# Taking the last layer of one half and the first layer of the next in turn, in a four-layer graph network on one core

## The reference, cut to what matters

```python
h = maximum(layernorm(x), 0); x = x + L0(h, adj)   # attention: e = leaky(s1_i + s2_j), masked softmax, times h W
h = maximum(layernorm(x), 0); x = x + L1(h, adj)   # attention on edge scores (h*a) h^T, softmax, times h
h = maximum(layernorm(x), 0); x = x + L2(h, adj)   # sum over relations of (mask_r h) W_r, plus bias
h = maximum(layernorm(x), 0); x = x + L3(h, adj)   # as L0, then elu
```

## Time and profile before

| | us |
|---|---|
| median of 3 runs | 293.67 |
| lowest and highest | 293.42, 294.1 |
| the profiled execution | 293.83 |
| its span, first to last instruction | 292.0 |
| PE busy in it | 276.5 |
| ACT busy | 257.4 |
| DVE busy | 251.2 |
| POOL busy | 237.4 |

### The profile page before, as it was taken

One profiled execution on the slowest core, in us unless ns is written; L12 is line 12 of the kernel. 1 busy time (PEld: TensorE's weight loads), 2 busy tenths in 40 slices (PEclk: granted clock), 3 DMA queues, 4 the chain that ended last, 5 costly groups with the idle time before them and its releaser, 6 DMA issues.

```text
span 292.0 us, 8093 instructions
## 1 busy us (share of the span) xinstructions
PE 276.5 (95%) x2250; PEld 257.6 (88%) x2250; DVE 251.2 (86%) x1211; ACT 257.4 (88%) x850; POOL 237.4 (81%) x382
## 2 busy tenths in 40 slices
PE   1899999999999999999899999999999999999991
PEld 1799998899889999999878999989888999999991
DVE  2689998998988767999998799999898886799995
ACT  3799998899998887897999889799999988789993
POOL 6999875777657999999999887768765699999932
PEclk9999999999999999999999999999999999999998
DMA  7935554500000000012121470000000000001123
GB/s 198 324 80 185 179 169 142 137 28 1 2 0 3 0 2 3 2 36 75 36 75 37 125 276 2 3 0 2 1 2 1 3 0 0 2 4 37 56 90 113
DMA packets 15950, 17.79 MB, mean 61 GB/s; under 512 B 2720, under 2 KB 11808, under 8 KB 15904
## 3 DMA queue, kind: packets, MB, share of 16 engines
q1 hardware_dynamic: 15488, 17.18, 18.5%
q10 hardware_dynamic: 416, 0.07, 0.1%
HBM read 13.05 MB, written 4.19 MB: 59 GB/s over the span
## 4 chain that ended last, share of the span: by engine, by line
PE 77%; DVE 10%; ACT 7%; issue 2%; DMA 2%; POOL 1%; SPq 0%; ACTq 0%; DVEq 0%; POOLq 0%
PE bank L972 23%; PE bank L914 9%; PE bank L919 9%; PE bank L890 7%; PE bank L848 6%; PE bank L957 5%; PE bank L939 5%; PE bank L927 4%; PE bank L969 3%; DVE pT L675 3%; PE bank L921 2%; DVE expy L709 2%; PE bank L874 2%; DVE result L718 2%; DMA edges<-in_adj 2%
## 5 line engine op out<-in xcount | busy, mean ns | idle before, releaser
L354 POOL TENSOR_TENSOR rs<-mv,minus_half 128x2 f32<-128x2 f32 x128 | 92.5, 723 | 41.4 <-DVE mv L619 41.2
L972 PE MATMUL bank<-val,pT 128*128 128x129 f32 x512 | 74.6, 275 | 0.0
L972 PEld LDWEIGHTS bank<-val,pT 128*128 128x128 f32 x512 | 67.8, 193 | 0.0
L368 POOL TENSOR_TENSOR h<-h,rs 128x256 f32<-128x256 f32 x96 | 59.7, 621 | 0.2
L675 DVE SCALAR_TENSOR_TENSOR pT<-bank,val,edgesT 128x256 f32<-128x256 f32 x128 | 55.0, 470 | 1.9 <-issue 1.0
L608 DVE BATCH_NORM_STATS2 st<-x 128x6 f32<-128x128 f32 x192 | 43.5, 267 | 0.0
L511 ACT ACTIVATE val<-bank,val 128x128 f32<-128x128 f32 x128 | 42.4, 406 | 0.1
L890 PE MATMUL bank<-w_gat,hT 128*128 128x131 f32 x256 | 41.0, 284 | 0.6 <-ACT hT L479 0.6
L848 PE MATMUL bank<-ident,h 128*128 128x128 f32 x192 | 38.2, 281 | 1.9 <-POOL h L368 1.5
L362 POOL TENSOR_TENSOR h<-x,mv 128x256 f32<-128x256 f32 x64 | 39.7, 621 | 0.0
L969 PE MATMUL bank<-ident,vsum 128*128 128x128 f32 x128 | 35.5, 277 | 1.4 <-DVE x L701 0.8
(11 more groups left out here) (84 smaller groups left out, 661.5 us busy)
## 6 DMA issues: line engine op xcount, KB each, us to landing
edges<-in_adj SPq DMA_DIRECT2D x32, 256.0 KB, 3.7
xin<-in_x SPq DMA_DIRECT2D x32, 128.0 KB, 2.7
out_x<-result SPq DMA_DIRECT2D x32, 128.0 KB, 1.7
w_rel<-in_L_gnn_weight SPq DMA_DIRECT2D x1, 256.0 KB, 2.9
w_gat<-in_L_gnn_W ACTq DMA_DIRECT2D x1, 64.0 KB, 2.6
w_gat<-in_L_gnn_W SPq DMA_DIRECT2D x1, 64.0 KB, 3.4
a_rel<-in_L_gnn_a SPq DMA_DIRECT2D x4, 0.5 KB, 3.4
bias<-in_L_gnn_bias SPq DMA_DIRECT2D x1, 64.0 KB, 3.1
```

The costliest lines, as they stand in the source:

```text
L354: pool.tensor_tensor(rs[:, g % WIDE], mv[:, g % WIDE, :, 1], minus_half[:, :], ALU.pow).then_inc(rs_ready, 1)
L368: pool.tensor_tensor(h[:, n % HS, :, 0:D], h[:, n % HS, :, 0:D], rs[:, g % WIDE, :].rearrange("p (t o) -> p t o", o=1).to_broadcast([P, T, ...
L972: last = pe.matmul(bank_o(n)[:, t], pT[:, n % 4, u, t * P:(t + 1) * P], values[:, u], start=(u == 0 and layer == 1), stop=(u == T - 1), sk ...
```

## The change

`ORDER` is new in its middle. Layers 0 to 2 of graphs 0 to 15 stand as before, and layers 1 to 3 of graphs 16 to 31. Between them came 16 units of layer 3 and then 16 of layer 0; now come (3,0), (3,1), and then in turn two units of layer 3 and two of layer 0, (3,2) (3,3) (0,16) (0,17) (3,4) (3,5) (0,18) (0,19) and so on, with (0,30) (0,31) last. `BEHIND` = 2 says how far layer 3 leads.

Since units of two halves are now mixed, slots that went by graph go by unit: st, mv, rs, nb, rinv, sums by n % WIDE, val by n % SLOTS, expy and relu_y by the count of layer 3 units, hsum and vsum by `gat_slot(n)`. The third bank of O is given only where seven units of layer 3 stand in a row, thus in the last stage alone. `residual` of layer 0 in graphs 16 to 31 gets a wait for the result of the graph whose x1 it overwrites. The lists of stages of PE, ACT, DVE and POOL have new lags and a new order; SP's lags grow from 10 to 12.

```diff
+BEHIND = 2
-ORDER = [(layer, first + k) for first in range(0, B, WIDE) for layer in range(4) for k in range(WIDE)]
+ORDER = [(layer, k) for layer in range(3) for k in range(WIDE)] + [(3, k) for k in range(BEHIND)]
+for k in range(0, WIDE, 2):
+    if k + BEHIND < WIDE:
+        ORDER += [(3, k + BEHIND), (3, k + BEHIND + 1)]
+    ORDER += [(0, WIDE + k), (0, WIDE + k + 1)]
+ORDER += [(layer, WIDE + k) for layer in range(1, 4) for k in range(WIDE)]
-LAG_MAX = 13
-SP_LAG = 10
+LAG_MAX = 15
+SP_LAG = 12
-        third = layer == 3 and (n + 6 >= len(ORDER) or ORDER[n + 6][0] == 3)
+        third = all(later == 3 for later, _ in ORDER[n:n + 7])
+def gat_slot(n):
+
+    return (nth(GATS, n) - 1) % SLOTS
...
-                pool.tensor_tensor(rs[:, g % WIDE], mv[:, g % WIDE, :, 1], minus_half[:, :], ALU.pow).then_inc(rs_ready, 1)
+                pool.tensor_tensor(rs[:, n % WIDE], mv[:, n % WIDE, :, 1], minus_half[:, :], ALU.pow).then_inc(rs_ready, 1)
...
                 src = xin[:, g % XS] if layer == 0 else x1[:, g % WIDE]
-                for t in range(T):
-                    last = dve.scalar_tensor_tensor(x1[:, g % WIDE, t], bank_o(n)[:, t, 0:D], rinv[:, g % WIDE, t:t + 1],
+                if layer == 0 and g >= WIDE:
+                    dve.wait_ge(result_ready[g % 2], (g - WIDE) // 2 + 1)
+                for t in range(T):
+                    last = dve.scalar_tensor_tensor(x1[:, g % WIDE, t], bank_o(n)[:, t, 0:D], rinv[:, n % WIDE, t:t + 1],
                                                     src[:, t], ALU.mult, ALU.add)
...
-            pipeline([(put_o, 8, LAST), (put_o, 8, FIRST), (put_z, 6, RGCN_REL), (put_z, 5, MULTI_REL),
+            pipeline([(put_v, 5, LAST), (put_v, 5, FIRST), (put_z, 6, FIRST), (put_z, 6, RGCN_REL),
```

More of the change, by code:

```diff
@@ L457, in normalize @@
                 for t in range(T):
-                    last = act.activation(h[:, n % HS, t, 0:D], x1[:, g % WIDE, t], ACT.Relu, bias=nb[:, g % WIDE, t:t + 1],
-                                          scale=rs[:, g % WIDE, t:t + 1])
+                    last = act.activation(h[:, n % HS, t, 0:D], x1[:, g % WIDE, t], ACT.Relu, bias=nb[:, n % WIDE, t:t + 1],
+                                          scale=rs[:, n % WIDE, t:t + 1])
                 last.then_inc(h_ready, 1)
@@ L510, in scale_v @@
                 for t in range(T):
-                    last = act.activation(val[:, k, t, 0:D], bank_v(n)[:, t, 0:D], ACT.Copy, scale=val[:, k, t, D:D + 1])
+                    last = act.activation(val[:, n % SLOTS, t, 0:D], bank_v(n)[:, t, 0:D], ACT.Copy, scale=val[:, n % SLOTS, t, D:D + 1])
                 last.then_inc(v_ready, 1)
@@ L549, in elu_parts @@
                 for t in range(T):
-                    act.activation(expy[:, n % 4, t], bank_o(n)[:, t, 0:D], ACT.Exp, scale=rinv[:, g % WIDE, t:t + 1])
-                    last = act.activation(relu_y[:, n % 4, t], bank_o(n)[:, t, 0:D], ACT.Relu, scale=rinv[:, g % WIDE, t:t + 1])
+                    act.activation(expy[:, (nth(LAST, n) - 1) % 4, t], bank_o(n)[:, t, 0:D], ACT.Exp, scale=rinv[:, n % WIDE, t:t + 1])
+                    last = act.activation(relu_y[:, (nth(LAST, n) - 1) % 4, t], bank_o(n)[:, t, 0:D], ACT.Relu, scale=rinv[:, n % WIDE, t:t + 1])
                 last.then_inc(y_ready, 1)
[L554 to L557, removed]
-                      (elu_parts, 9, LAST), (mask_edges, 4, FIRST), (scale_hT, 4, MULTI_REL),
-                      (exponentials, 6, MULTI_REL)])
+            pipeline([(take_edgesT, 5, FIRST), (scale_v, 6, LAST), (take_hT, 4, FIRST),
+                      (scale_v, 6, FIRST), (take_hT, 4, MULTI_REL), (take_hT, 4, LAST),
+                      (take_pT, 8, MULTI_REL), (mask_edges, 3, FIRST), (exponentials_of_s, 5, FIRST),
+                      (scale_hT, 4, MULTI_REL), (exponentials_of_s, 5, LAST), (take_mh, 6, RGCN_REL),
+                      (elu_parts, 9, LAST), (normalize, 4, RGCN_REL), (exponentials, 6, MULTI_REL),
+                      (upper_part, 5, MULTI_REL)])
             act.wait_ge(flag_ready, 1)
@@ L607, in statistics @@
                 for t in range(T):
-                    last = dve.bn_stats(st[:, g % WIDE, t, 0:6], src[:, t])
+                    last = dve.bn_stats(st[:, n % WIDE, t, 0:6], src[:, t])
                 last.then_inc(stats_ready, 1)
@@ L867, in put_edgesT @@
                 before = [m for m in THIRD if m < n]
-                if before and g % WIDE == 0:
+                if before and g % WIDE == 0 and before[0] < n:
                     pe.wait_ge(y_ready, nth(LAST, before[-1]))
@@ L892, in put_v @@
                 if k % VB == VB - 1:
-                    last = pe.matmul(bank_vsum(n), w_gat[layer // 3][:, 0:D], hsum[:, k - VB + 1:k + 1], start=True, stop=True)
+                    last = pe.matmul(bank_vsum(n), w_gat[layer // 3][:, 0:D], hsum[:, gat_slot(n) - VB + 1:gat_slot(n) + 1], start=True, stop=True)
                 last.then_inc(v_put, 1)
@@ L974, in put_o @@
                 last.then_inc(o_put, 1)
-            pipeline([(put_o, 8, LAST), (put_o, 8, FIRST), (put_z, 6, RGCN_REL), (put_z, 5, MULTI_REL),
-                      (put_o, 8, RGCN_REL), (put_edgesT, 5, FIRST), (put_hT, 3, MULTI_REL),
-                      (put_z, 5, FIRST), (put_pT, 7, MULTI_REL), (put_v, 4, FIRST), (put_o, 8, MULTI_REL),
-                      (put_hT, 3, FIRST), (put_hT, 3, LAST), (put_v, 4, LAST), (put_z, 5, LAST)])
+            pipeline([(put_v, 5, LAST), (put_v, 5, FIRST), (put_z, 6, FIRST), (put_z, 6, RGCN_REL),
+                      (put_z, 6, LAST), (put_z, 5, MULTI_REL), (put_o, 8, RGCN_REL),
+                      (put_pT, 7, MULTI_REL), (put_o, 8, FIRST), (put_edgesT, 4, FIRST), (put_o, 8, LAST),
+                      (put_hT, 3, FIRST), (put_hT, 3, MULTI_REL), (put_o, 8, MULTI_REL), (put_hT, 3, LAST)])
             pe.wait_ge(flag_step, 2)
```

60 lines of the change are left out of this document (30 added, 30 removed).

## The result

The changed kernel takes 291.93 us (median of 20 runs, 291.35 to 293.9) against 293.95 for the kernel before (20 runs on the same chips, 293.24 to 294.71): a ratio of 0.9931, 95% interval 0.9919 to 0.9942. It is 2.0 us faster; the prediction was 6.0 us less, 287.7, with a range from 285.9 to 290.4. The profiled span fell from 292.0 to 289.8 us.

What follows compares the result with a forecast made beforehand. PE was held by 5.7 us of waits where layer 3 turns into layer 0, chiefly for ACT; span 292.0 - 4.6 (middle) - 0.7 (first crossing) - 0.7 (start) = 286.0, + 1.83 - 0.16 = 287.7 us, range 285.9 to 290.4.

Steps and rivals of the forecast that it cites:

- step 1: Middle, ACT: four passes take 7.72 us where PE needs 8.78, so ACT stops being the limit.
- Step 2: Middle, loads: edges and x are fetched earlier, edges about 15 us ahead against 3.7 to landing; both waits go.
- Step 3: Middle, DVE: slightly slower than PE, costing PE 1.1 us (bounds 0 and 3.0), so the middle gains 4.6 of 5.7.
- DVE blocked by GpSimd: Rival, middle: every elu of 16 layer 3 units blocked, 6.4 us more on DVE, time 292.3 us; chance 8%.
- Two banks: slower: Rival: without the third bank, layer 3's put_o waits for elu_parts; at 0.5 us per unit, 294.6 us; chance 7%.
- Step 4: Middle: layer 0's residual in graphs 16 to 31 waits until add_x or add_x_odd has read x1; costed at nothing.
- Step 5: First half, layer 0 to 1: PE's wait behind DVE's weight checks eases; gain 0.7 us (bounds 0 and 0.9).
- Other layers keep the same cycle: Outside the middle each engine's cycle stays; one tighter place, normalize in layer 2, costed at nothing.
- Step 6: Start: mask_edges falls into ACT's idle time; gain 0.7 us, bounds a loss of 0.4 and a gain of 1.1.

Runs made afterwards that it cites:

- lists_alone: The changed kernel with the `ORDER` and third-bank rule of the kernel before, keeping the new lists and lags; 297.49 us, 1.0115 of the kernel before.
- light_gpsimd: The changed kernel with GpSimd's subtract_mean and scale_deviation on 2 of 128 columns for the 32 middle units; 289.07 us, 0.9852 of the kernel before.
- narrow_elu: The changed kernel with DVE's elu of graphs 0 to 15 working on 4 of 256 columns; 290.0 us, 0.9863 of the kernel before.
- check_later: The changed kernel with the weight checks on DVE moved from unit (1,0) to unit (1,6); 291.46 us, 0.9914 of the kernel before.
- dve_pool_before: The changed kernel with the lists and lags of DVE and GpSimd of the kernel before; 293.24 us, 0.9957 of the kernel before.

## Why the prediction was wrong

**Bound of the kernel before, and step 1, ACT.** Right. ACT's waits for loads and the holes from 148 to 172 went away with the order alone.

**Step 2, loads.** Right in its result: no load is waited for in the middle after. It has edges of graph 24 fetched when (0,16) is done with its residual; in the kernel it is when (0,16) is masked. lists_alone shows that distance is not all: a store that waits for a late add_x holds up every load behind it in SP's queue. The kernel before had this too (a store went out at 162.26, after add_x, and the load of x behind it then waited for a residual until 163.6).

**Step 3, DVE. This is the step that failed**: "What PE still loses I bound by 0 (all absorbed) and 3.0 (none); nearer to the first ... I take 1.1." The gap left is 3.37, so the middle gave 2.3 instead of 4.6. DVE's plain load was not what was missed: with GpSimd's work cut the same DVE instructions leave 0.33. What I left out is that elu and add_x have no fixed cost. GpSimd needs 0.57 + 0.57 + 0.66 us for a unit's subtract, scale and rs, 1.8 us, and layer 2's units take PE 1.3; so it enters layer 3 behind and works without a pause from 95.3 to 128.5. In that run elu and add_x were held, 1.07 and 0.76 us above their costs in the earlier trace rows, on a DVE that has, by the prediction's estimate, about 2 us of slack, all at one place. Before, with DVE's old list, elu was held for 1.24 us too, at 149.8, where ACT was the limit anyway.

**The rival "DVE blocked by GpSimd"** was this mechanism, given 8%. It said 292.3 and was nearest, but that is luck in part, since its account was wrong: a flat 0.40 for each of 16 elu, 6.4 us on DVE. (Less the slack of 1 that is 5.4, not the 4.6 it went on with.) GpSimd's full-size work cost 2.3 to 2.9 us (light_gpsimd), which bounds the lock. Of 14 elu from 122 to 177 one is held for 1.49 us and one for 0.66; the others last 0.38 to 0.57. I argued against the rival that the number of two-input instructions had not changed. The number is not what counts, but where they fall against GpSimd's instructions.

The Trainium skill ("SBUF — State Buffer", section "Who interferes with whom") states that a DVE instruction with two SBUF inputs contends with a GpSimd instruction that reads SBUF, and that one with at most one SBUF input, outside the modes that use both of DVE's ports, does not. The rows above agree in both: elu and add_x can be held (1.49 and 1.57 us), take_rows is not (0.85). So engines do not meet at semaphores alone, as the section on the core has it.

How long a hold lasts has no one answer in these traces. At 125.04 of narrow_elu it went over two full-size GpSimd instructions on end, 1.23 us for 0.14 us of work. But at 169.59 of the changed kernel add_x was let in between two of them, and the second of these, subtract_mean, lasted 0.79 us instead of 0.61:

```profile
169.59 0.49 DVE L731 TENSOR_TENSOR result<-expy,x 128x256 f32<-128x256 f32 x1
```

```profile
169.19 0.61 POOL L379 TENSOR_TENSOR h<-h,rs 128x256 f32<-128x256 f32 x1
169.77 0.79 POOL L373 TENSOR_TENSOR h<-xin,mv 128x256 f32<-128x256 f32 x1
```

This changed kernel has two holds over more than one full-size instruction, at 124.61 and 127.19, and several cases like the one at 169.59. Nor does a run without a pause decide it: in the last stage GpSimd has worked without one for 38 us when elu at 270.86 lasts 0.48.

**"Two banks: slower"** is refuted by the result, which is faster than before, and by light_gpsimd, which leaves 0.33 us with two banks. The waits for relu_y that it foretold are there, as the way in which DVE's lateness reaches PE.

**Step 4, the new wait.** Nothing in the trace waits at L714 for a result. It was not tried without it.

**Step 5, first crossing into layer 1.** Cause right, size wrong: forecast 0.7, measured 0.84 - 0.70 = 0.14. The wait of the earlier trace rows is gone, and smaller ones stand at 53 to 56. check_later shows that the weight checks make them: with the checks moved 0.00 is left. The forecast of 0.7 left out DVE's new list: in dve_pool_before, with DVE's and GpSimd's old ones, the whole 0.84 is gained.

**"Other layers keep the same cycle"** was the second step that failed: it costed the second crossing at nothing, and this lost 0.99 - 0.03 = 0.96 us.

**Step 6, the start.** The first put_o was to come at 15.3 and came at 15.40, against 16.02 before. But in the profiled runs of kernels with ACT's old list it lies at 15.71 to 16.29 (three), and with the new one at 15.40 to 16.07 (nine) and once at 17.92. A gain of 0.7 is not borne out; the means without that one differ by 0.2.

**Sum.** 287.7 + 2.3 for the middle + 1.0 for the second crossing + 0.6 for the first + 0.5 for the start = 292.1, against 291.93. The 0.5 takes the start's gain as the 0.2 of the means; in the one pair of profiles it was 0.62. So 2.3 of the 4.2 us missed are step 3, and the small terms are known to some tenths only.

**Open**: why a two-input instruction is let in at one place and held over two or more GpSimd instructions at another was seen and not tested, and what at the second crossing could be moved was not tried.

## What to carry to other kernels

Two engines that lock each other have no fixed price per instruction: look in the trace at which of the one's instructions are held and beside what, and try the places where the other waits. Here moving elu, add_x and the weight checks gained another 2.7 to 2.9 us, more than the 2.0 of the whole reordering. A new order and new lists have to be judged apart: the order alone gave 1.4 us, the lists alone cost 3.5 (about half of it the clock, by the estimate above), together they gave 2.0. A stop of PE can cost more than its length: look at the granted clock behind it before a time is put down to an edit. And when a load is shifted, look at the entrance and the exit of the stretch, not only at its steady pace.

## What the runs showed of the hardware

A DVE instruction with two SBUF inputs can be held over two or more successive full-size GpSimd instructions: a 4-column one took 1.23 us for 0.14 (narrow_elu), a 256-column one up to 1.89 for 0.40 (lists_alone). It can also be let in between two of them (169.59 of the changed kernel), and the second GpSimd instruction then lasts 0.79 instead of 0.61 us.

A held one can come through beside GpSimd's 2-column pow, which then lasts 0.87 us instead of 0.69 (125.78 of the changed kernel). The pow does not always leave room: in the earlier trace rows add_x lasts 0.82 us beside it.

In lists_alone, PE stood still for 3.13 us at the full granted clock, and was granted about half of it for some 3.4 us of its work after that. In dve_pool_before a half clock (0.50 from 184 to 187) came behind two us in which PE was busy for 0.2.
